# A graph network on one core: edge ranking in PSUM, counting shared with ScalarE, empty slots spread over many rows

## The chip, the cores and the metric

The kernel runs on one core of a Trainium2 chip. The metric is the device time of one execution in microseconds. Engines are named as in the profile: PE is TensorE, DVE is VectorE, ACT is ScalarE, POOL is GpSimd, SP is SyncE, which issues most transfers. An indirect DMA (a gather or a scatter with one row index per partition) is issued by POOL.

## What is computed

A graph of 6250 nodes with 64 features and 200000 edges, sorted by their target `dst`, goes through four blocks, each on a normalised copy of the node rows and added to them. Cut to what matters:

```python
h = relu(layernorm(x)); x = x + L0(h, W, b, edge_weight, src, dst)   # 3 hyperbolic GCN layers
h = relu(layernorm(x)); x = x + L1(h, edge_attr_16, ...)             # attention over edges
h = relu(layernorm(x)); x = x + L2(h, edge_attr_8, ...)              # edge MLP
h = relu(layernorm(x)); x = x + L3(h, ...)                           # attention over edges
# every block gathers node rows by src and sums over dst, for instance
msgs = edge_weight[:, None] * ht[src]
agg = segment_sum(msgs, dst, num_segments=6250)
```

So there are six passes over the edges: three GCN layers, attention, MLP, attention.

## The kernel before

**Buckets and groups.** The nodes are cut into T = 49 tiles of 128. An edge belongs to the bucket `dst >> 7`; bucket 49 takes the 704 entries that fill 200000 edges up to 128 x KC = 128 x 1568. Inside the chip the edges are sorted again by bucket (the kernel doesn't rely on their order), and each bucket is rounded up to groups of GE = 256 slots. NG = 832 groups are worked on. A slot that holds no edge has target NO_DST, which matches no node, and weight 0; its source is a node that doesn't exist, NO_SRC = 52 x 128 - 1, one row of the table for all empty slots.

**The sort**, in order. DVE fills a tile `fill` with empty slots, and SP writes it 42 times over the DRAM array `packed` (L283). The bucket of each edge is in `bucket`, 128 x 1568, in SBUF. *Counting* (L440 to L445): 50 times, once for each bin, DVE compares `bucket` with the bin and adds up along the row, into `cnt`. PE turns the counts into prefixes, and DVE into `base`, the next free position of each bin on each partition. *Ranking* (L474 to L497): the 1568 columns are done in portions of PLACED = 7, 14, 14, 14 units of 32 columns. For each portion 50 bins are gone through, five operations each: compare (a mask), running sum that starts at `base` (tensor_tensor_scan), its last column back to `base`, compare and multiply with the running sum, add to `rank`. Four closing operations turn the ranks into row numbers `pos`, and `pos_made` goes up.

**The scatter.** SP waits for `pos_made` of a portion and loads slabs of 16 columns of the payload and of `pos` (L292 to L301), two slabs in turn, each again when its 16 scatters have landed. POOL waits for all 42 fills and then scatters column by column into `packed`, 1568 indirect DMAs of 128 rows (L343). Meanwhile DVE does what comes before the first pass: the marks of the groups' first elements in RES (49 scalar_tensor_tensor of 832 columns), the layer input, the rows of layer 0. When all scatters have landed, SP loads `packed` in 42 pieces and DVE unpacks them. Then the first pass can begin.

**A pass.** POOL gathers the table rows of 256 slots by two indirect DMAs a group (L362), into a ring of 16 groups; SP loads the indices for 8 groups at a time, when the gathers of the turn before have landed. DVE makes one-hot matrices, PE multiplies them with the rows, and DVE adds the product to the node tile's sums ACC (L734 in GCN and MLP passes, L737 in attention passes). The loop has 16 groups a turn. Positions ascend with the bucket, so the groups that are left over at the end of the 832 hold empty slots alone.

## Time and profile before

| | us |
|---|---|
| median of 3 runs | 19662.9 |
| the runs | 19653.38 to 19730.66 |
| the profiled execution, its span | 16151.0 |
| POOL busy in it | 11150.9 (69%) |
| PE busy | 8811.1 (55%) |
| DVE busy | 8667.7 (54%) |
| ACT busy | 3544.5 (22%) |

The span reaches from the first to the last instruction of the profiled execution; the device times of the runs lie 3512 us above it, and the profile doesn't show what that is. The sort and the unpacking take the first 2569 us of the span, the six passes with the node work between them the rest. Busy shares are means over stages with different limits, so each stage has to be read by itself. POOL's time is almost all indirect DMAs, 1568 scatters and 9984 gathers.

### The profile page before, as it was taken

Reading aid. Unit: us, or ns where it says so; the run is one execution under the profiler, and the core shown is the slowest. Engines: PE = TensorE matmul, PEld = TensorE weight load, DVE = VectorE, ACT = ScalarE, POOL = GpSimd, SP = SyncE. Lnnn points to the kernel's source line nnn. Section 1 sums busy time; section 2 is a strip of 40 time slices with the busy share of each in tenths; the row PEclk is TensorE's granted clock in tenths of the full one; section 3 lists DMA queues with packets and bytes.
Section 4 is the critical chain, followed back from the end, with each engine's and each line's share of the span. In section 5 each row is a group of like instructions: output and inputs, shape, how many; then the busy total and the mean of one; then the engine's idle time right before and its main releaser. Section 6 shows DMA issues by size and latency. Waiting matters only on the chain.

```text
span 16151.0 us, 291712 instructions
## 1 busy us (share of the span) xinstructions
PE 8811.1 (55%) x60538; PEld 7573.0 (47%) x60539; DVE 8667.7 (54%) x38886; ACT 3544.5 (22%) x11877; POOL 11150.9 (69%) x11556
## 2 busy tenths in 40 slices
PE   0000002444434444434444488888699999788887
PEld 0000002333333333333333377777577777677777
DVE  8820004333343333343333488888766666688887
ACT  0000000000000000000000166666422222466665
POOL 3877774777747777747777477777477777477776
PEclk9965555555555555555555555555555555555555
DMA  2001113111121111221111211111211112211113
GB/s 86 20 24 26 26 31 83 27 27 27 27 21 27 27 27 27 26 23 27 27 27 27 22 27 26 26 26 26 21 27 27 26 26 26 20 28 27 27 27 27
DMA packets 509319, 465.87 MB, mean 29 GB/s; under 512 B 299149, under 2 KB 324301, under 8 KB 507854
## 3 DMA queue, kind: packets, MB, share of 16 engines
q0 software_dynamic: 369664, 358.70, 17.2%
q1 hardware_dynamic: 139086, 102.30, 2.2%
q14 instruction: 543, 4.45, 0.1%
q8 instruction: 26, 0.43, 0.0%
HBM read 389.08 MB, written 65.20 MB: 28 GB/s over the span
## 4 chain that ended last, share of the span: by engine, by line
PE 36%; DVE 23%; issue 21%; POOL 12%; DVEq 5%; DMA 3%; ACT 0%; POOLq 0%; ACTq 0%; SPq 0%
PE bank L1170 18%; POOL packed L343 10%; DVE OH L613 7%; PE bank L1269 6%; PE bank L1271 3%; DMA G<-table,idx 3%; DVE r_gm L646 2%; PE bank L1209 2%; PE bank L1282 2%; POOL G L362 2%; DVE ACC L734 1%; PE bank L1220 1%; PE bank L1232 1%; DVE ACC L737 1%; DVEq L596 1%
## 5 line engine op out<-in xcount | busy, mean ns | idle before, releaser
L362 POOL DMA_INDIRECT G<-table,idx x9984 | 9480.9, 950 | 4211.3 <-issue 2234.3
L1170 PE MATMUL bank<-G,OH 128*128 128x64 f32 x9984 | 2715.8, 428 | 5397.7 <-DVE OH L613 2605.1
L1170 PEld LDWEIGHTS bank<-G,OH 128*128 128x128 f32 x9984 | 2314.8, 322 | 5798.6 <-DVE OH L613 2897.2
L734 DVE TENSOR_TENSOR ACC<-ACC,bank 128x64 f32 (+1 forms) x3328 | 734.8, 221 | 3703.4 <-PE bank L1170 3701.6
L343 POOL DMA_INDIRECT packed<-Y,slab_pos x1568 | 1669.8, 1065 | 736.4 <-issue 494.7
L613 DVE TENSOR_SCALAR OH<-const,DL,W 128x128 f32<-128x128 f32 x4992 | 1740.1, 398 | 421.9 <-PE bank L1170 353.0
L1017 ACT ACTIVATE n_res<-n_arg 128x52 f32<-128x52 f32 x25 | 6.2, 246 | 8303.3 <-DVE n_arg L538 8179.8
L1170 PE MATMUL bank<-ZR,OH 128*128 128x65 f32 x6656 | 1765.4, 419 | 0.0
L1170 PEld LDWEIGHTS bank<-ZR,OH 128*128 128x128 f32 x6656 | 1623.9, 334 | 0.2
L1232 PE MATMUL bank<-ER,OHT 128*128 x9984 | 994.7, 174 | 751.1 <-DVE negm_lo L675 563.4
L1232 PEld LDWEIGHTS bank<-ER,OHT 128*128 128x128 bf16 x9984 | 781.8, 104 | 1048.5 <-issue 920.1
L1269 PE MATMUL bank<-WE,E8T 16*128 16x64 f32 x3328 | 1140.3, 443 | 41.6 <-ACT E8T L1092 41.4
L1220 PE MATMUL bank<-const,V 128*128 128x128 f32 x3328 | 1115.2, 439 | 21.9 <-ACT V L1072 21.8
L1209 PE MATMUL bank<-ident_b,OHB 128*128 128x128 bf16 x4992 | 1033.9, 311 | 39.1 <-DVE OHB L624 39.1
L624 DVE TENSOR_TENSOR OHB<-iota_b,DLw 128x256 bf16<-128x256 bf16 x2496 | 1051.4, 421 | 6.4 <-issue 6.4
L1269 PEld LDWEIGHTS bank<-WE,E8T 16*128 16x128 f32 x3328 | 828.1, 308 | 194.8 <-issue 50.4
L1047 ACT ACTIVATE OHT<-bank,const 128x256 bf16<-128x256 f32 x1664 | 785.2, 472 | 528.9 <-PE bank L1209 494.2
L1065 ACT ACTIVATE OH<-OHB,const 128x256 f32<-128x256 bf16 x1664 | 825.6, 496 | 41.1 <-DVE OHB L624 22.7
L417 DVE TENSOR_SCALAR W<-Z 128x40 f32 x42 | 8.1, 194 | 1494.7 <-DMA Z<-packed 1493.9
L1209 PEld LDWEIGHTS bank<-ident_b,OHB 128*128 128x128 bf16 x4992 | 656.2, 145 | 143.6 <-DVE OHB L624 39.9
L646 DVE TENSOR_REDUCE r_gm<-bank 128x1 f32<-128x256 f32 x1664 | 696.0, 418 | 9.1 <-PE bank L1220 8.8
L1047 ACT ACTIVATE OHT<-bank 128x256 bf16<-128x256 f32 x832 | 318.6, 383 | 1726.0 <-PE bank L1262 1722.0
(220 smaller groups left out, 14865.0 us busy)
## 6 DMA issues: line engine op xcount, KB each, us to landing
G<-table,idx POOLq DMA_INDIRECT x9984
packed<-Y SPq DMA_DIRECT2D x42, 640.0 KB, 17.5
Z<-packed SPq DMA_DIRECT2D x42, 640.0 KB, 3.7
Y<-in_payload SPq DMA_DIRECT2D x98, 256.0 KB
packed<-Y,slab_pos POOLq DMA_INDIRECT x1568
table<-Y SPq DMA_DIRECT2D x6, 1690.0 KB, 5.4
idx<-SRC SPq DMA_DIRECT2D x624, 8.0 KB
X<-in_x SPq DMA_DIRECT2D x1, 1568.0 KB, 8.7
```

The costliest lines, as they stand in the source:

```text
L343: pool.indirect_dma_start(out=packed_rows, out_offset=bass.IndirectOffsetOnAxis(ap=slab_pos[:, h, c:c + 1], axis=0), in_=slab[:, h, c, :], ...
L362: pool.indirect_dma_start(out=G[:, 2 * q + c, :], out_offset=None, in_=table, in_offset=bass.IndirectOffsetOnAxis(ap=idx[:, h, j:j + 1], a ...
L613: o = v.tensor_scalar(OH[:, q, c, :], iota, DL[:, at], W[:, at], ALU.is_equal, ALU.mult)
L624: v.tensor_tensor(OHB[:, q, :, :], iota_b[:, :].unsqueeze(1).to_broadcast([P, 2, P]), DLw[:, 2 * u:2 * u + 2].unsqueeze(2).to_broadcast([P ...
L646: v.tensor_reduce(sr["gm"][:, r:r + 1], ps_x[r % 2][:, 0:GE], AX.X, ALU.max).then_inc(a_done, 1)
L734: v.tensor_tensor(acc[:, 0:w], acc[:, 0:w], ps_a[r % 2][:, 0:w], ALU.add).then_inc(acc_done, 1)
L1047: return a.activation(OHT[:, r, :], ps_m[r % 2][:, 0:GE], ACT.Identity, scale=scale, bias=bias)
L1170: o = pe.matmul(ps_a[r % 2][:, 0:w], OH[:, q, c, :], parts[c], start=c == 0, stop=c == 1)
L1209: o = pe.matmul(ps_m[r % 2][:, c * P:(c + 1) * P], OHB[:, q, c, :], ident_b[:, :], start=True, stop=True)
L1220: o = pe.transpose(ps_x[r % 2][:, c * P:(c + 1) * P], V[:, r % 4, c, :], ident)
L1232: pe.matmul(e[:, c:c + 1], one, ER3[:, bass.ds(t, 1), k], start=k == 0, stop=k == 2)
L1269: pe.matmul(ps_e[r % 2][:, c * D:(c + 1) * D], E8T[:, r % 4, :], WE[:, c, :], start=True, stop=False)
```

## The change

Three things, in one edit. *Counting*: DVE counts the first 22 bins as before. ACT takes the other ACT_BINS = 28: it sums, in 29 passes over `bucket`, the sign of (middle of a bin - bucket), and half the difference of two such sums is the count of the bin between. *Ranking*: the mask and the running sum now lie in two PSUM banks instead of SBUF; `bucket` and `rank` stay in SBUF. A bank has 512 columns, so the portions are at most 480, and the first ones are small: PLACED = 2, 3, 5, 9, 15, 15. *Empty slots*: their source is one of the 384 nodes of the three tiles beyond the last, by partition and column, in `fill` and in the payload's last entries. Since these numbers come with the constants, the fill waits for them, and some clearing moves behind it.

```diff
-PLACED = [7, 14, 14, 14]
+PLACED = [2, 3, 5, 9, 15, 15]
+ACT_BINS = 28
...
-NO_SRC = TP * P - 1
+PAD_TILES = TP - T
...
-            sp.wait_ge(fill_made, 2)
+            sp.wait_ge(fill_made, 1)
...
-            sp.wait_ge(fill_made, 1)
+            sp.wait_ge(fill_made, 2)
...
             own.count(v.memset(y_flat[:, 0:PACK * PAY], 0.0))
-            own.wait()
-            own.count(v.memset(fill[:, :, SRC_AT:SRC_AT + 1].bitcast(I32), NO_SRC))
+            v.memset(WE[:, :, :], 0.0).then_inc(fill_made, 1)
+            own.wait()
+            v.wait_ge(s_const, 16)
+            for k in range(PAD_TILES):
+                to = fill[:, k:PACK:PAD_TILES, SRC_AT].bitcast(I32)
+                own.count(v.tensor_copy(to, pad_nodes[:, k:k + 1].to_broadcast([P, len(range(k, PACK, PAD_TILES))])))
+            own.wait()
             v.memset(fill[:, :, DST_AT:DST_AT + 1].bitcast(I32), NO_DST).then_inc(fill_made, 1)
-            v.memset(WE[:, :, :], 0.0).then_inc(fill_made, 1)
             own.count(v.memset(X[:, T:TP, :], 0.0))
             own.count(v.memset(sched[:, :], 0))
             own.count(v.memset(rank, 0.0))
-            v.wait_ge(s_const, 16)
...
-            with v.Fori(0, NB) as b:
+            with v.Fori(0, low) as b:
...
+            v.wait_ge(signs_summed, ACT_BINS + 1)
+            tt(cnt[:, low:NB], sums[:, low:NB], sums[:, low - 1:NB - 1], ALU.subtract)
+            ts(cnt[:, low:NB], cnt[:, low:NB], 0.5, None, ALU.mult)
...
+                ps_mask, ps_scan = bank[3][:, 0:c1 - c0], bank[4][:, 0:c1 - c0]
...
-                    ts(mask[:, here], bucket[:, here], one, None, ALU.is_equal)
+                    ts(ps_mask, bucket[:, here], one, None, ALU.is_equal)
                     own.wait()
-                    own.count(v.tensor_tensor_scan(scan[:, here], ones[:, 0:1].to_broadcast([P, c1 - c0]), mask[:, here],
+                    own.count(v.tensor_tensor_scan(ps_scan, ones[:, 0:1].to_broadcast([P, c1 - c0]), ps_mask,
                                                    carry, ALU.mult, ALU.add))
                     own.wait()
-                    own.count(move(carry, scan[:, c1 - 1:c1]))
-                    stt(mask[:, here], bucket[:, here], one, scan[:, here], ALU.is_equal, ALU.mult)
-                    tt(rank[:, here], rank[:, here], mask[:, here], ALU.add)
+                    own.count(move(carry, ps_scan[:, c1 - c0 - 1:c1 - c0]))
+                    stt(ps_mask, bucket[:, here], one, ps_scan, ALU.is_equal, ALU.mult)
+                    tt(rank[:, here], rank[:, here], ps_mask, ALU.add)
...
+            a.wait_ge(s_const, 16)
+            a.wait_ge(bucket_made, 1)
+            for j in range(ACT_BINS + 1):
+                b = NB - ACT_BINS - 1 + j
+                need(a, signs_summed, j - 1)
+                a.activation(signs[:, j % 2, :], bucket, ACT.Sign, scale=-1.0, bias=mids[:, b:b + 1],
+                             accum_out=sums[:, b:b + 1]).then_inc(signs_summed, 1)
...
+    c[:, C_PAD:C_PAD + PAD_TILES] = np.arange(T * P, TP * P).reshape(PAD_TILES, P).T
+    c[:, C_MID:C_MID + NB] = np.arange(NB) + 0.5
...
-    payload[N_EDGES:, SRC_AT] = NO_SRC
+    payload[N_EDGES:, SRC_AT] = T * P + np.arange(P * KC - N_EDGES) % (PAD_TILES * P)
```

On DVE, one turn of the loop over the bins in the first portion, before (EA8 is the memory in which `bucket`, the mask, the running sum and `rank` lie; a scan is listed as a SCALAR_TENSOR_TENSOR):

```order
L405 TENSOR_SCALAR EA8<-EA8,const 128x224
L74 REGISTER_ALU
L482 ISA [waits dve_done]
L482 SCALAR_TENSOR_TENSOR EA8<-const,base,EA8 128x224
L74 REGISTER_ALU
L417 TENSOR_SCALAR base<-EA8 128x1 [waits dve_done]
L74 REGISTER_ALU
L409 SCALAR_TENSOR_TENSOR EA8<-EA8,const 128x224 [waits dve_done]
L74 REGISTER_ALU
L401 TENSOR_TENSOR EA8<-EA8 128x224 [waits dve_done]
```

The same turn in the changed kernel:

```order
L413 TENSOR_SCALAR bank3<-EA8,const 128x64
L77 REGISTER_ALU
L498 ISA [waits dve_done]
L498 SCALAR_TENSOR_TENSOR bank4<-const,base,bank3 128x64
L77 REGISTER_ALU
L425 TENSOR_SCALAR base<-bank4 128x1 [waits dve_done]
L77 REGISTER_ALU
L417 SCALAR_TENSOR_TENSOR bank3<-EA8,const,bank4 128x64 [waits dve_done]
L77 REGISTER_ALU
L409 TENSOR_TENSOR EA8<-EA8,bank3 128x64 [waits dve_done]
```

The order is the same; the mask moved to bank 3 and the running sum to bank 4, and the portion shrank from 224 to 64 columns.

On ACT, the start of its stream, before (fn_arg is DVE's request for a function on node values):

```order
L1017 ACT_TABLE_LOAD
L1017 ACTIVATE hb_r<-hb_arg 128x3 [waits fn_arg]
L1017 ACT_TABLE_LOAD
L1017 ACTIVATE hb_t<-hb_norm 128x3 [waits fn_arg]
L1017 ACT_TABLE_LOAD
```

And in the changed kernel:

```order
L1122 ACT_TABLE_LOAD [waits bucket_made]
L1122 ACTIVATE EA8,sums<-EA8,const 128x1568 [waits s_const]
L1122 ACTIVATE EA8,sums<-EA8,const 128x1568
L1122 ACTIVATE EA8,sums<-EA8,const 128x1568 [waits signs_summed] x27
L1033 ACT_TABLE_LOAD
L1033 ACTIVATE hb_r<-hb_arg 128x3 [waits fn_arg]
```

The 29 sums stand ahead of all that ACT did, and start when DVE has made the buckets; DVE waits for them ahead of the prefixes.

## Rows read from the trace of the kernel before

**Rows 1.** The page's head and its chain that ended last, by engine.

```profile
span 16151.0 us, 291712 instructions
PE 36%; DVE 23%; issue 21%; POOL 12%; DVEq 5%; DMA 3%; ACT 0%; POOLq 0%; ACTq 0%; SPq 0%
```

**Rows 2.** Windows: stretch, length, busy of PE, PEld, DVE, ACT, POOL; clock, DMA, GB/s.

```profile
110.00:237.00 127.00, 2.20 (x10) 2.00 (x10) 105.42 (x270) 0.00 (x0) 0.00 (x0) 1.00 0.00 0
...
570.00:740.00 170.00, 0.00 (x0) 0.00 (x0) 150.74 (x247) 0.00 (x0) 138.99 (x100) 1.00 0.08 20
...
1100.00:2400.00 1300.00, 0.00 (x0) 0.00 (x0) 0.00 (x0) 0.00 (x0) 976.49 (x1021) 0.50 0.11 26
```

**Rows 3.** First count in time; by form: compares of two widths, one from PSUM.

```profile
8.08 1.84 DVE L443 TENSOR_SCALAR_CACHE_REDUCE EA<-EA,const 128x1568 f32<-128x1568 f32 x1 [0.20 <-DVE EA L436]
...
L405 DVE TENSOR_SCALAR EA<-EA,const 128x224 f32<-128x224 f32 x50 | 16.8, 336 | 7.6 <-DVE EA L401 7.5
...
L405 DVE TENSOR_SCALAR EA<-EA,const 128x448 f32<-128x448 f32 x98 | 44.5, 454 | 14.8 <-DVE EA L401 14.8
...
L417 DVE TENSOR_SCALAR ACC<-bank 128x256 f32 x12 | 5.1, 425 | 18.5 <-PE bank L1152 18.5
```

**Rows 4.** Timeline (start, duration, what): count done, ranking, second portion, scatters.

```profile
110.17 0.19 DVE L447 COPY base<-cnt 128x50 f32<-128x50 f32 x1
...
114.98 0.34 DVE L405 TENSOR_SCALAR EA<-EA,const 128x224 f32<-128x224 f32 x1
...
236.84 0.45 DVE L405 TENSOR_SCALAR EA<-EA,const 128x448 f32<-128x448 f32 x1
...
242.19 1.12 POOL L343 DMA_INDIRECT packed<-Y,slab_pos  x1 [241.72 <-DMA slab_pos<-EA]
...
2405.76 0.96 POOL L343 DMA_INDIRECT packed<-Y,slab_pos  x1 [0.30 <-issue]
```

**Rows 5.** Timeline and groups: indirect DMAs beside DVE work with different operands.

```profile
833.69 3.63 DVE L401 TENSOR_TENSOR U<-X,n_a 128x3328 f32<-128x3328 f32 x1
833.97 4.17 POOL L343 DMA_INDIRECT packed<-Y,slab_pos  x1 [0.31 <-issue]
...
L409 DVE SCALAR_TENSOR_TENSOR RES<-V,cum,RES 128x832 f32<-128x832 f32 x49 | 54.5, 1113 | 6.5
...
L343 POOL DMA_INDIRECT packed<-Y,slab_pos x45 | 43.8, 974 | 15.1 <-issue 15.1
...
4520.55 0.94 POOL L362 DMA_INDIRECT G<-table,idx  x1 [0.30 <-PE bank L1170]
4520.62 0.22 DVE L734 TENSOR_TENSOR ACC<-ACC,bank 128x64 f32 x1 [1.58 <-PE bank L1170]
```

**Rows 6.** ACT groups by form, whole span: count, busy and mean ns, idle before.

```profile
L1065 ACT ACTIVATE OH<-OHB,const 128x256 f32<-128x256 bf16 x1664 | 825.6, 496 | 41.1 <-DVE OHB L624 22.7 <-PE bank L1170 18.4
...
L1072 ACT ACTIVATE V<-OHB,G 128x128 f32<-128x128 bf16 x1664 | 564.6, 386 | 29.9 <-DMA G<-table,idx 28.3 <-PE bank L1220 1.6
```

**Rows 7.** ACC on DVE: windows (busy, clock, DMA, GB/s), then its attention timeline.

```profile
4590.00:4673.00 83.00, 5.32 (x24) 0.50 0.89 19
4300.00:4383.00 83.00, 7.32 (x33) 0.50 0.19 27
...
11640.00:13690.00 2050.00, 174.39 (x790) 0.50 0.18 27
13715.00:13790.00 75.00, 6.59 (x30) 0.50 0.76 16
...
11417.12 0.28 DVE L737 SCALAR_TENSOR_TENSOR ACC<-ACC,r_corr,bank 128x65 f32 x1
11425.73 0.28 DVE L737 SCALAR_TENSOR_TENSOR ACC<-ACC,r_corr,bank 128x65 f32 x1
...
11460.88 0.28 DVE L737 SCALAR_TENSOR_TENSOR ACC<-ACC,r_corr,bank 128x65 f32 x1
...
11484.35 0.28 DVE L737 SCALAR_TENSOR_TENSOR ACC<-ACC,r_corr,bank 128x65 f32 x1
```

More of the change, by code:

```diff
@@ L58 @@
 assert STEPS_N % 2 == 1
-assert sum(PLACED) * 2 * SLAB == KC and NS % PACK == 0 and (NS // PACK) % 2 == 0 and KC % (2 * SLAB) == 0
+assert max(PLACED) * 2 * SLAB <= 512 and sum(PLACED) * 2 * SLAB == KC and NS % PACK == 0 and (NS // PACK) % 2 == 0 and KC % (2 * SLAB) == 0
 assert NS * P >= NG * GE + P * KC - N_EDGES + GE and P * SCHED >= NG + BODY
 C_ID, C_TRI, C_IOTA, C_ONE, C_BIN, C_GRP = 0, P, 2 * P, 3 * P, 4 * P, 4 * P + NB
-C_ALL = C_GRP + SCHED
+C_PAD = C_GRP + SCHED
+C_MID = C_PAD + PAD_TILES
+C_ALL = C_MID + NB
 B_GCN, B_BIAS, B_GAMMA, B_BETA, B_B1, B_B2, B_BIAS3 = 0, 3, 4, 5, 6, 7, 8
@@ L114, in build @@
         ea8_flat = EA8[:, :, :].rearrange("p s c -> p (s c)")
-        bucket, mask, scan, rank, posf = (ea8_flat[:, i * KC:(i + 1) * KC] for i in range(5))
+        bucket, mask, signs, rank = (ea8_flat[:, i * KC:(i + 1) * KC] for i in range(4))
+        signs = signs.bitcast(BF16).rearrange("p (h c) -> p h c", h=2)
         dst_raw = ea8_flat[:, 5 * KC:6 * KC].bitcast(I32)
@@ L130, in build @@
         grp_i = sb("grp_i", [P, NB], I32)
+        sums = sb("sums", [P, NB])
         before = sb("before", [P, SCHED, T])
@@ L139, in build @@
         bins, groups = const[:, C_BIN:C_BIN + NB], const[:, C_GRP:C_GRP + SCHED]
+        pad_nodes = const[:, C_PAD:C_PAD + PAD_TILES]
+        mids = const[:, C_MID:C_MID + NB]
         ident_b = sb("ident_b", [P, P], BF16)
@@ L209, in build @@
         counted, prefixes = sem("counted"), sem("prefixes")
+        bucket_made, signs_summed = sem("bucket_made"), sem("signs_summed")
         sched_made, sched_stored, sched_loaded = sem("sched_made"), sem("sched_stored"), sem("sched_loaded")
@@ L435, in _ @@
             own.wait()
-            own.count(v.tensor_scalar(bucket, pos_hi, float(T), None, ALU.min))
+            v.tensor_scalar(bucket, pos_hi, float(T), None, ALU.min).then_inc(bucket_made, 1)
+            v.wait_ge(bucket_made, 1)
+            low = NB - ACT_BINS
             at0 = own.n
-            with v.Fori(0, NB) as b:
+            with v.Fori(0, low) as b:
                 own.n = b + at0
@@ L444, in _ @@
                                           accum_out=cnt[:, bass.ds(b, 1)]))
-            own.n = at0 + NB
+            own.n = at0 + low
+            v.wait_ge(signs_summed, ACT_BINS + 1)
+            tt(cnt[:, low:NB], sums[:, low:NB], sums[:, low - 1:NB - 1], ALU.subtract)
+            ts(cnt[:, low:NB], cnt[:, low:NB], 0.5, None, ALU.mult)
             own.wait()
```

## Prediction

> **What bounds the kernel now.** I read the page's head and its chain first. The profiled span is 16151.0 us and no engine owns the chain: PE, DVE, POOL and plain issue share it [rows 1]. The change touches two stretches only, so the question is what ends last in each, and the busy shares say nothing on that. The median of the runs is 19662.9 us, 3512 us above the span; nothing in the trace lies in those 3512 us. I make the sum on the span and take the rest as it is, with one rival for the case that it isn't.
>
> The first stretch is the sort. Read the windows in order. GpSimd's scatter of the payload starts at 242.19 and its last one at 2405.76; only then does SyncE load the packed edges, and the passes come after that [rows 4]. From 1100 on VectorE does nothing [rows 2]. So the stretch is: when the first scatter starts, plus 1568 scatters at their pace. The pace has two values: 1021 scatters in 1300 us where VectorE is idle, 1.273 us each, and 100 in 170 us while VectorE ranks, 1.70 us each [rows 2]. At 1.273 us throughout, 1567 steps would take 1995 us; they took 2163.6, so 168 us are lost to VectorE's work. The 519 us of ranking after 242 hold 305 scatters at 1.70, 0.427 us too many each: 130 us. The other 38 us belong to work after the ranking, which stays.
>
> The second stretch is the end of each of the six passes. Each pass takes 832 groups of 256 slots. 200000 edges fill 782 groups, and each of 49 buckets rounds up by half a group on average, so some 25 groups at the end hold empty slots alone, all pointing at one row of the table. There the sums on ACC come 24 times in 83 us against 33 times before, and the DMA share is 0.89 against 0.19 [rows 7].
>
> **The change, part by part.** *Counting.* It begins at 8.08 and its result is copied at 110.17: 50 bins at 2.04 us, of which 1.84 is the operation [rows 3, 4]. VectorE keeps 22, 45 us. It starts later, since the clearing of rank and two smaller ones now stand behind the wait for the constants: I allow 3 us for them, so 11 to 56. ScalarE does 29 passes over 1568 columns, a form that isn't in the trace. Its forms with a pointer bias take 386 ns for 128 columns and 496 ns for 256 [rows 6]: 0.86 ns a column, so 496 + 1312 x 0.86 = 1.62 us, plus a gap and a read of the accumulator of 0.1 to 0.3 us as VectorE shows (2.04 against 1.84). I take 1.8: 29 are 52 us, with a table load the count ends near 65, and ScalarE is the later of the two. The bounds are 56 (ScalarE hidden behind VectorE) and 80 (2.3 us each). Two small operations more, then as before 4.81 us to the ranking [rows 4]: it starts at 70.3, not at 114.98, 44.7 us earlier.
>
> The Trainium skill, ScalarE: Activation LUTs, section What ACT_TABLE_LOAD costs, gives an activation with pointer bias about 280 ns + 0.833 ns a column: an estimate of 1.59 us, by which the count would end some 6 us sooner. No row here shows it at this width.
>
> *Ranking.* Before, a bin over 224 columns takes (236.84 - 114.98 - 1.3)/50 = 2.41 us (1.3 for the four closing operations) and over 448 columns 3.44, 247 instructions at five a bin in 170 us [rows 2, 4]: 1.37 us + 4.62 ns a column. With PSUM the compare loses its speed: it takes 336 ns and 454 ns in SBUF, 0.53 ns a column; the nearest tensor_scalar with a PSUM operand takes 425 ns for 256 columns, at best 1.06 ns a column [rows 3]. Slope 5.15 ns. For the fixed part that row shows nothing extra; I take 1.42 us, bounds 1.37 and 1.70. Portions of 64, 96, 160, 288, 480, 480 columns give 1.75, 1.91, 2.24, 2.90, 3.89, 3.89 us a bin, thus 87, 96, 112, 145, 195, 195 us, 830 in all with 6 us of closing work, against some 647 before. Those 190 us more of VectorE lie beside the scatters: ranking ends near 906 and what follows is done well before the scatters are. The cover is over 1000 us.
>
> That the compare slows is what the rows show; VectorE: DVE Perf Modes of the Trainium skill, section Why PSUM operands drop a tier, states it as a rule, and it speaks against the change. By it and by the row the first portion is 64 x 0.53 x 50 = 1.7 us longer than in SBUF; only the sum over all columns, 42 us, would hurt, and that is covered.
>
> *First scatter.* The first positions come at 70.3 + 87 + 1 = 158.8, and the scatter starts 5.35 us behind them as before (236.84 to 242.19 [rows 4]): 164.2, a gain of 78 us.
>
> *Starving.* 64 columns keep GpSimd busy for 81.5 us, to 245.7. The next positions come at 158.8 + 97 = 255.8, and with 5.35 us for the loads GpSimd waits 15.4 us. The 96 columns then last until 383; the third positions come at 369, so nothing is waited for, with 9 us to spare; later portions have more. Cost 15 us, bounds 0 and 45 (fixed part at 1.70 us a bin: both gaps open).
>
> *The pace beside the ranking.* A tensor_tensor of 3.63 us with both inputs in SBUF holds a scatter that began behind it for 4.17 us, to 0.82 us after its end. But 49 scalar_tensor_tensor with both inputs in SBUF leave 45 scatters at 974 ns. An ACC sum with one input in PSUM runs inside a gather of 0.94 us and adds nothing [rows 5]. In the new ranking no operation has two tensor inputs in SBUF and the compare doesn't write SBUF. So I take 1.273: the 130 us go. The bounds are 0 and 130; I am near the upper one since the PSUM row is the same kind of operation.
>
> SBUF — State Buffer in the Trainium skill, section Who interferes with whom, says that an operation with at most one SBUF input outside the two-port modes doesn't contend with GpSimd. By that rule the 130 us go too. It also counts any operation with two SBUF inputs as contending; the 974 ns row doesn't bear that out.
>
> *Empty slots.* In a GCN pass 3.46 us a group against 2.52 over some 26 groups: 25 us, three times 75 [rows 7]. In an attention pass the last but one turn of the loop has a gap of 23.5 us between ACC sums where others have 8.6 (11417.12 to 11425.73): 15 us [rows 7]; the other such pass has the same shape, I take 13. In the MLP pass 30 sums in 75 us against 790 in 2050 [rows 7]: nothing to win. Together 103 us. The fill gets three small operations more, hidden: GpSimd waits for its transfers too, but from 110 us on the DMAs carry nothing [rows 2], and the first scatter comes 54 us later still.
>
> **Sum.** 78 + 130 - 15 = 193 for the sort and 103 for the slots: 296 us. Span 15855, time 19367.
>
> **Rivals.** *The contention stays* (PSUM doesn't keep VectorE out of GpSimd's way, or it is the compare or the scan that blocks in any place). Then scatters run at 1.70 for 906 - 164 = 742 us: 436 of them, 186 us lost, no starving. The sort gains 78 + 130 - 186 = 22, with the slots 125: 19538. Against it stand the ACC rows, for it that these are short, 0.22 us.
>
> *Scatters fall in step with the bins, and the kernel is slower.* Before, two scatters fit each bin of 3.44 us. If only one went through per bin, wherever its gap is, 742 us of ranking would hold 250 scatters: 742 - 250 x 1.273 = 424 us lost, the sort 216 us later, the whole 113 us slower after the slots: 19776. It decides from a mean pace of 2.2 us on. The widest bins, 3.9 us, are where it would show. Against it: even a fully blocked scatter ends 0.82 us after the blocker [rows 5], and no blocker of that length is left.
>
> *The slots win nothing*, since the slow pace at the end has another cause: 193 us, 19470. The DMA share of 0.89 at 19 GB/s against 27 [rows 7] speaks against it: slower descriptors, not more bytes.
>
> *The 3512 us lie in the indirect DMAs*: over 11552 of them, 0.30 us each. Then gathers set 3.1 us a group everywhere, the slots win about 10 us a pass, and the blocking may be partly hidden: 105 to 240 us, say 19490.
>
> **Chances.** Forecast 0.68; contention stays 0.10; slots nothing 0.07; time in the DMAs 0.11; slower 0.04. For the range: at the top 19540, which takes in the first, third and fourth rival; at the bottom, if the gain grows with 19663/16151, 360 us: 19300. Faster or slower counts from 0.5%, 98 us, about what a measurement of this kernel can tell from no change. Below 19565 lie the forecast, two rivals whole and most of the others: 0.92; within 0.05; slower 0.03.
>
> **What would show it.** First scatter near 164, one gap of about 15 us some 80 us later, then about 0.96 us a scatter all through the ranking, last scatter near 2213. ScalarE's passes near 1.6 to 1.8 us. No rise of the DMA share at the ends of the passes, ACC sums at 2.5 us there. Wrong if scatters still take 1.3 to 1.5 us beside the ranking, if GpSimd waits at the third portion too, or if span and time don't shrink alike.

## The result, and the profile after

| | us |
|---|---|
| before, median of 4 runs beside the changed kernel | 19659.8 |
| changed kernel, median of 4 runs | 19877.2 (19836.6 to 19897.2) |
| ratio, 95% interval | 1.0088 (1.0061 to 1.0115) |
| profiled execution of the changed kernel | 19862.0, span 19860.2 |

Predicted were 19367 us and a range of 19300 to 19540: 296 us less. It is 217 us more.

One thing has to be said first, since no number can be read without it: chips differ. On some, the kernel before takes 16.1 ms, on others 19.7 to 19.9 ms, and its span is then as long as its time. I call them **A chips** and **B chips**. The trace of before [rows 1 to 7] is from an A chip, the times under it from B chips, and so is the result. What the prediction called "3512 us above the span" lies inside the span of a B chip. Only kernels on chips of one kind are compared below.

Head and chain of the page after (against [rows 1]), two of its groups, and what GpSimd's scatters waited for from 100 to 2650 us (waited for, sum, times, longest):

```profile
span 19860.2 us, 293015 instructions
...
PE 19%; another core or an unknown queue 17%; issue 11%; DVE 11%; DVEq 4%; ACT 2%; ACTq 0%; DMA 0%; POOL 0%; SPq 0%; POOLq 0%
...
L370 POOL DMA_INDIRECT G<-table,idx x9984 | 9619.5, 963 | 7595.1 <-issue 2888.1
L750 DVE TENSOR_TENSOR ACC<-ACC,bank 128x64 f32 (+1 forms) x3328 | 732.2, 220 | 5514.6 <-remote 3968.0
...
POOL packed L351 <- DMA slab_pos<-EA: 491.4, 5, 158.8
```

Five waits for positions where I forecast two. The first, 158.8 us, is the time to the first scatter; the other four are 333 us, and I had allowed 15.

The timeline of VectorE and ScalarE after, where the count ends and ranking starts (start, duration, engine, what, idle before):

```profile
52.13 0.08 DVE L455 DVE_READ_ACCUMULATOR EA<-EA,const  x1
53.26 1.59 ACT L1122 ACTIVATE EA<-EA,const 128x1568 bf16<-128x1568 f32 x1
54.75 0.19 ACT L1122 ACTIVATION_READ_ACCUMULATOR EA<-EA,const 128x1 f32 x1
54.84 1.59 ACT L1122 ACTIVATE EA<-EA,const 128x1568 bf16<-128x1568 f32 x1
...
56.55 0.19 DVE L409 TENSOR_TENSOR cnt<-sums 128x28 f32<-128x28 f32 x1 [2.30 <-ACT EA L1122]
...
61.79 0.29 DVE L413 TENSOR_SCALAR bank<-EA,const 128x64 f32<-128x64 f32 x1
...
159.25 1.12 POOL L351 DMA_INDIRECT packed<-Y,slab_pos  x1 [158.78 <-DMA slab_pos<-EA]
```

Up to here all is as forecast, 5 us early. Now the second portion (96 columns), first while the scatters have just begun, then 40 us later:

```profile
172.32 0.32 DVE L413 TENSOR_SCALAR bank<-EA,const 128x96 f32<-128x96 f32 x1 [0.46 <-issue]
174.50 0.32 DVE L413 TENSOR_SCALAR bank<-EA,const 128x96 f32<-128x96 f32 x1 [0.46 <-DVE EA L409]
178.45 0.32 DVE L413 TENSOR_SCALAR bank<-EA,const 128x96 f32<-128x96 f32 x1 [2.23 <-issue]
...
211.38 0.32 DVE L413 TENSOR_SCALAR bank<-EA,const 128x96 f32<-128x96 f32 x1 [4.08 <-issue]
214.74 0.42 DVE L498 TENSOR_TENSOR_SCAN bank<-const,base,bank 128x96 f32<-128x96 f32 x1 [3.04 <-issue]
216.14 0.16 DVE L425 TENSOR_SCALAR base<-bank 128x1 f32 x1 [0.98 <-DVE bank L498]
217.54 0.32 DVE L417 SCALAR_TENSOR_TENSOR bank<-EA,const,bank 128x96 f32<-128x96 f32 x1 [1.24 <-issue]
218.95 0.25 DVE L409 TENSOR_TENSOR EA<-EA,bank 128x96 f32<-128x96 f32 x1 [1.08 <-issue]
223.98 0.32 DVE L413 TENSOR_SCALAR bank<-EA,const 128x96 f32<-128x96 f32 x1 [4.77 <-issue]
```

The compare comes again after 2.18 us at 174.50 and after 12.60 us at 223.98. The operations are as long as before (0.32, 0.42, 0.16); what grew is the idle time ahead of them, put down to "issue": nothing that the profile shows was waited for. (This trace holds 98480 records of semaphore updates where that of [rows 1] has 255417, and so it is with every trace of a B chip. So the names of what ended a wait are less sure here, and I go by the starts.) When GpSimd has run out of positions (from 239 to 326.8), VectorE is back at 2.2 us a bin. So the small portions make GpSimd wait, its waiting frees VectorE, and its next scatters hold VectorE again.

### The profile page after: what moved, and what is told of

It is laid out like the page before. It is cut to its first block, busy times and chain, and to the rows that moved or that the text cites. A ratio compares the mean times of both kernels' runs of the same rounds, so it can differ in the third digit from the quotient of the medians.

```text
span 19860.2 us, 293015 instructions
## 1 busy us (share of the span) xinstructions
PE 9006.6 (45%) x60538; PEld 7528.7 (38%) x60539; DVE 8505.1 (43%) x39342; ACT 3392.3 (17%) x11936; POOL 11213.2 (56%) x11556
## 4 chain that ended last, share of the span: by engine, by line
PE 19%; another core or an unknown queue 17%; issue 11%; DVE 11%; DVEq 4%; ACT 2%; ACTq 0%; DMA 0%; POOL 0%; SPq 0%; POOLq 0%
PE bank L1193 6%; PE bank L1243 4%; PE bank L1255 3%; PE bank L1232 2%; PE bank L1292 2%; DVE OH L629 2%; DVEq L612 2%; PE bank L1259 1%; DVE OHB L640 1%; DVE r_gm L662 1%; PE bank L1294 1%; DVE ACC L753 1%; ACT V L1088 1%; DVE ACC L750 1%
## 5 line engine op out<-in xcount | busy, mean ns | idle before, releaser
L370 POOL DMA_INDIRECT G<-table,idx x9984 | 9619.5, 963 | 7595.1 <-issue 2888.1
L1193 PE MATMUL bank<-G,OH 128*128 128x64 f32 x9984 | 2599.3, 431 | 5022.8 <-DVE OH L629 2471.4
L1193 PEld LDWEIGHTS bank<-G,OH 128*128 128x128 f32 x9984 | 2265.0, 324 | 5357.1 <-DVE OH L629 2472.9
L351 POOL DMA_INDIRECT packed<-Y,slab_pos x1568 | 1593.5, 1016 | 998.4 <-issue 507.0
L629 DVE TENSOR_SCALAR OH<-const,DL,W 128x128 f32<-128x128 f32 x4992 | 1551.5, 359 | 516.5 <-issue 468.9
L1168 PE MATMUL bank<-const,st 128*64 128x128 f32 x728 | 146.3, 370 | 2277.7 <-ACT st L1042 2277.7
L1168 PEld LDWEIGHTS bank<-const,st 128*64 128x64 f32 x728 | 118.5, 191 | 2286.8 <-issue 2068.4
```

Source lines behind the costliest of these rows:

```text
L351: pool.indirect_dma_start(out=packed_rows, out_offset=bass.IndirectOffsetOnAxis(ap=slab_pos[:, h, c:c + 1], axis=0), in_=slab[:, h, c, :], ...
L370: pool.indirect_dma_start(out=G[:, 2 * q + c, :], out_offset=None, in_=table, in_offset=bass.IndirectOffsetOnAxis(ap=idx[:, h, j:j + 1], a ...
L629: o = v.tensor_scalar(OH[:, q, c, :], iota, DL[:, at], W[:, at], ALU.is_equal, ALU.mult)
L1193: o = pe.matmul(ps_a[r % 2][:, 0:w], OH[:, q, c, :], parts[c], start=c == 0, stop=c == 1)
```

## The experiments

All durations of a bin below are from start to start of its running sum. Each run's comparison is with the kernel before on the same chip.

**Each part alone, on an A chip** (before: 16135 us).

> The kernel before, unchanged, looked at once more. The trace that the prediction was made on has a span of 16151 us, while the runs took 19660; the changed kernel's span (19860) is its whole time. Theory A (engines are held at issue while GpSimd issues indirect DMAs, before the change too): the span is near 19650, the passes take 2400 us and more as in the changed kernel, and VectorE's ranking beside the scatters shows idle time put down to issue. Theory B (only the changed kernel has these idle times): the span is near 16150 again and the 3500 us lie outside it.

Measured: time 16099.4, span 16097.6 us, scatters from 241.5 to 2405.7. The trace of [rows 4] again, and no 3512 us beside the span.

> The kernel before with only the empty slots spread over 384 rows. Theory A (the end of each pass is held by one row): 103 us faster as predicted, 0.5%; less if all passes are slower than the trace of before showed, since then the tail is no slower than the rest: 0 to 60 us faster. Theory B (the slots are what slows the changed kernel): slower by some 200 us.

```diff
-    payload[N_EDGES:, SRC_AT] = NO_SRC
+    payload[N_EDGES:, SRC_AT] = T * P + np.arange(P * KC - N_EDGES) % (PAD_TILES * P)
```

Measured: ratio 0.9937 (0.9916 to 0.9957), 129 us by the medians, 90 between the two traces. Windows at the end of the first GCN pass, before and with the slots spread (columns as in [rows 2]):

```profile
4600.00:4660.00 60.00, 19.48 (x72) 16.68 (x72) 14.66 (x54) 0.00 (x0) 38.79 (x42) 0.50 0.87 20
```

```profile
4600.00:4660.00 60.00, 26.15 (x98) 22.32 (x98) 20.53 (x70) 0.00 (x0) 43.64 (x47) 0.50 0.17 26
```

The DMA share of 0.87 is gone and 47 gathers fit in 60 us where 42 did; in both windows the last 3 us hold no gather, as the pass has none left. More is won behind the last gather. Its issue and the last sum on ACC of this pass, before and with the slots spread:

```profile
4657.25 0.96 POOL L362 DMA_INDIRECT G<-table,idx  x1 [0.30 <-issue]
4676.50 0.22 DVE L734 TENSOR_TENSOR ACC<-ACC,bank 128x64 f32 x1 [2.65 <-PE bank L1170]
```

```profile
4656.71 0.94 POOL L364 DMA_INDIRECT G<-table,idx  x1 [0.30 <-issue]
4660.52 0.22 DVE L739 TENSOR_TENSOR ACC<-ACC,bank 128x64 f32 x1 [2.34 <-PE bank L1175]
```

The sum comes 19 us behind the gather in the first and 4 us in the second. From first gather to last sum the GCN passes take 22.7, 22.4 and 21.8 us less, 67 in all (forecast 75), the attention passes 27 and 24 (forecast 15 and 13), the MLP pass the same. The attention figures move by 15 us and more between kernels with the same slots. The forecast of 103 us lies between 129 and 90. What lies between the passes moves in steps of some 21 us from trace to trace and adds up to 560 to 624 us whatever the kernel, so two single spans can differ by some 60 us for that alone.

> The kernel before with only the mask and the running sum of the ranking in PSUM, portions of 224 and 448 columns kept. Theory A (port contention is what PSUM takes away): scatters beside the ranking take 0.96 us instead of 1.3 to 1.5, up to 130 us faster. Theory B (VectorE is held at issue beside the scatters, so GpSimd's pace no longer hangs on it): within 60 us of before.

```diff
-                    ts(mask[:, here], bucket[:, here], one, None, ALU.is_equal)
+                    ts(ps_mask, bucket[:, here], one, None, ALU.is_equal)
...
-                    tt(rank[:, here], rank[:, here], mask[:, here], ALU.add)
+                    tt(rank[:, here], rank[:, here], ps_mask, ALU.add)
```

Measured: 0.9929 (0.9906 to 0.9952), 130 us, last scatter at 2282.3. The timeline while scatters run:

```profile
699.47 0.69 DVE L405 TENSOR_SCALAR bank<-EA,const 128x448 f32<-128x448 f32 x1 [0.15 <-DVE EA L401]
700.29 1.15 DVE L483 TENSOR_TENSOR_SCAN bank<-const,base,bank 128x448 f32<-128x448 f32 x1
701.48 0.16 DVE L417 TENSOR_SCALAR base<-bank 128x1 f32 x1
701.67 0.69 DVE L409 SCALAR_TENSOR_TENSOR bank<-EA,const,bank 128x448 f32<-128x448 f32 x1
702.39 0.62 DVE L401 TENSOR_TENSOR EA<-EA,bank 128x448 f32<-128x448 f32 x1
703.17 0.69 DVE L405 TENSOR_SCALAR bank<-EA,const 128x448 f32<-128x448 f32 x1 [0.15 <-DVE EA L401]
```

A bin is 3.71 us and scatters pass at 1.27 each. From the first scatter to the last it is 2033.5 us, 2164.3 in e0: the 130 us of blocking are gone, and the rival "contention stays" is out. The first scatter comes 7 us later (248.8), which leaves 124 us at the first gather; the medians differ by 130, the two spans by 91.

> The kernel before with only the counting shared with ScalarE. The first scatter comes some 50 us earlier. Theory A: that goes through to the end, 50 us faster (0.25%). Theory B (what follows eats it): no difference, or slower.

```diff
-            with v.Fori(0, NB) as b:
+            with v.Fori(0, low) as b:
...
+            v.wait_ge(signs_summed, ACT_BINS + 1)
```

Measured: 0.9954 (0.9932 to 0.9975), 80 us; first scatter 187.0 in place of 241.5. The first gather comes 46 us earlier and the span is 57 us shorter, near the 44.7 us forecast; the 80 us of the medians are more than the trace accounts for, and the eight times spread over 125 us. So on an A chip each part wins about what its term said.

**The same chip, a B chip, for before, after and between** (before: 19938 us).

> The kernel before once more, for a trace from the same chip as the next three. Two conditions are known so far. In the one (16.1 ms for this kernel) the scatters run from 241.5 to 2359 or 2406 and VectorE's ranking bins over 448 columns take 3.44 us. In the other (19.66 ms) there is no trace of this kernel yet. My theory of it: while GpSimd issues indirect DMAs, the instructions of the other engines are held before they start. It expects ranking bins of 9 us or more once the scatters have begun, most of it as idle time put down to issue, and gather passes of 2.6 to 3.1 ms in place of 2.08. The rival, that each indirect DMA is simply 0.3 us longer on that chip, expects bins of 3.4 us and a uniformly slower scatter.

Measured: 19952.5, span 19950.7 us. Its groups beside the scatters, 240 to 2520 us, and the gathers:

```profile
L482 DVE TENSOR_TENSOR_SCAN EA<-const,base,EA 128x448 f32<-128x448 f32 x150 | 172.6, 1151 | 20.8
L409 DVE SCALAR_TENSOR_TENSOR RES<-V,cum,RES 128x832 f32<-128x832 f32 x49 | 53.7, 1096 | 131.8 <-issue 129.2
...
L362 POOL DMA_INDIRECT G<-table,idx x9984 | 9605.2, 962 | 7776.9 <-issue 2805.0
```

My theory of it failed in half. The passes are held: 2432 to 3193 us each where the A chip takes 2081 to 2254, in sum 16472 against 12780; that is nearly all of the 3853 us between the two spans. The 49 marks in RES are held too, 131.8 us of idle where the A chip shows 6.5 [rows 5]. But the ranking of the kernel before is not: bins of 3.47 us, on both kinds of chip alike. There the scatters, at 1.73 us, are the ones that are blocked.

> The changed kernel as it is. If this chip is one on which the kernel before takes 16.1 ms: the three parts alone gave 129, 130 and 80 us, so the whole should give about 300 us, 15830 us, ratio 0.981, with the last scatter near 2210 and at most 15 us of waiting GpSimd after the first portion. If it is one of 19.66 ms: ratio 1.009 again, because VectorE is held between its instructions while scatters are issued, and the small portions leave GpSimd without positions for some 330 us. The rival (the gather passes are what got slower, by the slots' table rows) expects the loss in the passes and not before 2600 us.

Measured: 1.0047 (1.0032 to 1.0062). Scatters from 159.2 to 2606.6, GpSimd waits 344 us after the first; ranking bins at 12.6 us beside the scatters, whatever their width.

> The changed kernel with the old portions of 224 and 448 columns; slots, PSUM and the shared count stay. Where before takes 16.1 ms: first scatter near 187, the sort some 20 us later than with small portions, 15850 us, ratio 0.982. Where it takes 19.66 ms: if the starved GpSimd is the cause of the loss, most of the 330 us come back, 19500 to 19600 us, ratio 0.992 to 0.997, and GpSimd waits for positions less than 100 us; if the loss lies elsewhere (the PSUM operands, the passes) the ratio stays at 1.009.

```diff
-PLACED = [2, 3, 5, 9, 15, 15]
+PLACED = [7, 14, 14, 14]
```

Measured: 0.9974 (0.9962 to 0.9986), 164 us better than the change. GpSimd still waits once after the first scatter, 101.6 us (295.7 less the 194.1 before any scatter), as the bins are held here too. Groups over 60 to 1250 us, and the waits:

```profile
L498 DVE TENSOR_TENSOR_SCAN bank<-const,base,bank 128x448 f32<-128x448 f32 x109 | 125.8, 1154 | 173.5 <-issue 167.9 <-DVE bank L413 0.6
L413 DVE TENSOR_SCALAR bank<-EA,const 128x448 f32<-128x448 f32 x109 | 74.9, 687 | 336.8 <-issue 330.7 <-DVE EA L409 6.1
...
POOL packed L351 <- DMA slab_pos<-EA: 295.7, 2, 194.1
```

Bins of 448 columns take 12.6 us, as those of 96 do. The width doesn't matter; so a portion costs 630 us beside scatters, and fewer portions mean less waiting.

> The kernel before with the small portions alone; rank through SBUF, VectorE counts all, the slots point at one row. Where before takes 16.1 ms: the first scatter comes at about 170 in place of 241.5 (-71), GpSimd waits once or twice for some 10 us, contention stays at 1.7 us a scatter over 250 us more of ranking: 50 to 70 us faster or nothing, ratio 0.995 to 1.000. Where it takes 19.66 ms: 300 to 400 us slower, ratio 1.015 to 1.02, if starving is the cause, since nothing else of the change is in it; 1.000 or below if the small portions are innocent.

The edit is the one line of e6, the other way round, on the kernel before. Measured: 1.0066 (1.0044 to 1.0087). So narrow bins are held without PSUM too: with everything in SBUF, bins of 96, 160 and 288 columns take about 12.6 us as well, and only those of 480 run at 3.61 with scatters at 1.8. Wide bins are another matter: over 448 columns they run at 3.47 us through SBUF (e4) and at 12.6 through PSUM (e6). Smaller portions alone make the kernel slower on a B chip.

**What in a bin is held.** The next four went first to an A chip (before: 16123 us), and show there what each is worth when nothing is held.

> The kernel before with the spread slots and the shared count, ranking as before (SBUF, portions of 224 and 448 columns). The theory is that only the ranking of the changed kernel loses where the kernel before takes 19.7 to 19.9 ms: there the first scatter comes 55 us earlier, ranking bins keep their 3.47 us and nothing is held, so 55 us from the count and some 20 to 30 from the slots: ratio 0.9960 (0.9945 to 0.9975). Where before takes 16.1 ms: 80 + 129 us less whatever the two share, ratio 0.987 to 0.990. The rival, that a held VectorE can come with any earlier start, expects bins of 12.6 us here as well and a ratio of 1.00.

Its edits are those of e1 and e3 together. Measured: 0.9875 (0.9849 to 0.9900).

> All three parts with portions of 224 and 448 columns, as in e6, but the 50 bins of a portion are written out one after the other, so that VectorE waits on constants and has no loop counter, no register and no branch there. In e6 on the chip of 19.9 ms each bin over 448 columns took 12.6 us in place of 3.8. If registers and branches are what is held: bins of 3.9 us, no waiting GpSimd, last scatter near 2180, ratio 0.984 to 0.987 against 0.9974. If every instruction that waits on and raises a semaphore is held, whatever it waits for: bins stay at 12.6 us, ratio 0.997. In between (the branch alone): the largest gap, before the compare, goes and bins take 8 to 9 us. Where before takes 16.1 ms nothing of this shows: bins 3.7 us, ratio 0.981 to 0.983 either way.

```diff
-                with v.Fori(0, NB) as b:
-                    own.n = b * 5 + at0
-                    one, carry = bins[:, bass.ds(b, 1)], base[:, bass.ds(b, 1)]
+                for b in range(NB):
+                    one, carry = bins[:, b:b + 1], base[:, b:b + 1]
```

Measured: 0.9826 (0.9803 to 0.9849); bins 3.48 us.

> The changed kernel with its small portions, bins written out as in e9. If registers and branches are held: bins of 1.8 to 4 us beside the scatters, GpSimd waits 15 us at the second portion as I had forecast, last scatter near 2160 and ratio 0.983 on the slower chip (the changed kernel had 1.0047 there). If every instruction is held: 1.005 again. Where before takes 16.1 ms: as the changed kernel, 0.981.

Measured: 0.9797 (0.9772 to 0.9822), 336 us, the best on an A chip. First scatter 140.5, one wait of 3.5 us after it, last scatter 2173.0.

> The kernel of e6 with a sixth instruction in each bin, a tensor_scalar over 128x1 that takes 0.16 us (it multiplies a used number by one into a tile that is no longer read). On the slower chip a bin of five took 12.6 us beside ten scatters. If each of VectorE's instructions costs two scatters or 2.5 us, a bin takes 15.1 us; if a bin is held as a whole, or by the branch alone, it stays at 12.6 to 12.8. Where before takes 16.1 ms the bin goes from 3.71 to 3.90 us.

```diff
+                    ts(grp[:, 0:1], cum[:, 0:1], 1.0, None, ALU.mult)
```

Measured: 15904 us, bins 4.09 us. Then a B chip (before: 19687 us).

> The changed kernel, which has been timed only where the kernel before takes 19.7 to 19.9 ms (1.0088 and 1.0047). Where before takes 16.1 ms nothing holds VectorE in the runs so far, and my sum for the span should stand there: 296 us less, 15.82 ms, ratio 0.9815 (0.978 to 0.985), first scatter at 159, GpSimd waits once for 5 to 20 us after it, last scatter near 2210. If this is a chip of 19.7 to 19.9 ms: ratio 1.003 to 1.010 for the third time.

Measured: 1.0092 (1.0075 to 1.0109), 194 us.

> The changed kernel with its ranking bins written out (e10 again; there 0.9797 where before takes 16.1 ms). On a chip of 19.9 ms: if registers and branches are what is held, bins of 1.6 to 3.6 us beside the scatters, GpSimd waits under 20 us, last scatter near 2170 to 2280, ratio 0.981 to 0.985. If every instruction that waits on and raises a semaphore is held, as long as in a loop: bins of 12.6 us, the starving stays and the ratio is 1.003 to 1.010.

Measured: 0.9950 (0.9927 to 0.9974), 83 us. Bins beside scatters 7.0 us; GpSimd waits 140 us in three waits after the first scatter, and the last scatter is at 2406.0.

> The same with portions of 224 and 448 columns (e9 again; 0.9826 where before takes 16.1 ms). On a chip of 19.9 ms: registers and branches held: bins of 3.5 us, no starving, ratio 0.984 to 0.987; every instruction held: bins of 12.6 us, 296 us of starving as in e6, ratio 0.997.

Measured: 0.9912 (0.9895 to 0.9930), 172 us, with bins of 7.0 us, no waiting after the first scatter and the last one at 2349.1. (The 296 us of e6 in this text count the wait for the first scatter too; 102 was meant.)

> e6 with a sixth instruction of 0.16 us in each bin (e11 again; there the bin went from 3.71 to 4.09 us, 0.38 for it with its wait). On a chip of 19.9 ms: 15.1 us a bin if each instruction costs about two scatters, 12.6 to 12.8 if the bin is held as a whole or by its branch.

Measured: 19757.9 us, bins of 14.0. The timelines of f3, then f4:

```profile
702.09 1.16 DVE L497 TENSOR_TENSOR_SCAN bank<-const,base,bank 128x448 f32<-128x448 f32 x1 [0.72 <-DVE bank L413]
703.48 0.16 DVE L425 TENSOR_SCALAR base<-bank 128x1 f32<-128x1 f32 x1 [0.23 <-DVE bank L497]
704.88 0.69 DVE L417 SCALAR_TENSOR_TENSOR bank<-EA,const,bank 128x448 f32<-128x448 f32 x1 [1.24 <-DVE base L425]
706.27 0.62 DVE L409 TENSOR_TENSOR EA<-EA,bank 128x448 f32<-128x448 f32 x1 [0.71 <-DVE bank L417]
707.69 0.69 DVE L413 TENSOR_SCALAR bank<-EA,const 128x448 f32<-128x448 f32 x1 [0.79 <-DVE EA L409]
```

```profile
702.77 1.16 DVE L498 TENSOR_TENSOR_SCAN bank<-const,base,bank 128x448 f32<-128x448 f32 x1 [2.74 <-issue]
704.17 0.16 DVE L425 TENSOR_SCALAR base<-bank 128x1 f32 x1 [0.24 <-issue]
705.58 0.69 DVE L417 SCALAR_TENSOR_TENSOR bank<-EA,const,bank 128x448 f32<-128x448 f32 x1 [1.25 <-issue]
706.98 0.62 DVE L409 TENSOR_TENSOR EA<-EA,bank 128x448 f32<-128x448 f32 x1 [0.71 <-issue]
709.08 0.15 DVE L413 TENSOR_SCALAR grp<-cum 128x1 f32<-128x1 f32 x1 [1.48 <-issue]
714.04 0.69 DVE L413 TENSOR_SCALAR bank<-EA,const 128x448 f32<-128x448 f32 x1 [4.81 <-issue]
```

Read the starts. In f3 they are 1.39, 1.40, 1.39, 1.42 us apart, though the operations last 1.16, 0.16, 0.69 and 0.62: nearly each of VectorE's instructions takes 1.40 us beside the scatters, and five of them 7.0. In f4's loop the distances are 1.40, 1.41, 1.40 and 2.10, and from the last operation over the branch to the next compare 4.96. In a turn of the loop with five operations nine further instructions stand (registers, the parts of the scan and compare that are issued apart, the branch); they make the bin 12.6 instead of 7.0, 5.6 us. The sixth operation, with one register instruction more, adds 1.40, not the 2.5 that I had put on it. So both of my readings were half right: every instruction is held, and those of the loop on top.

**The last two,** on another B chip (before: 19680 us).

> The changed kernel once more, for the case that the kernel before takes 16.1 ms on this chip: then my sum for the span is tested with nothing held. It gave 296 us less; e10, which differs in the written out bins alone, gave 336. Expected 290 to 310 us less, ratio 0.981 to 0.982, first scatter at 159, GpSimd waits 5 to 20 us after the first portion, last scatter near 2200. If before takes 19.7 to 19.9 ms: 1.005 to 1.009 again.

Measured: 1.0078 (1.0062 to 1.0095).

> Spread slots and shared count with the ranking of before (e8 again, 0.9875 where before takes 16.1 ms). If before takes 19.7 to 19.9 ms here: bins of 3.47 us, not held, and no starving; 55 us from the count and 20 to 40 from the slots, ratio 0.9950 to 0.9965, against 0.9974 for the three parts with large portions and 1.005 to 1.009 for the change as it is. If an earlier start alone brings the holding: bins of 12.6 us and 0.998 to 1.005. If before takes 16.1 ms: 0.9875 again.

Measured: 0.9966 (0.9944 to 0.9989), bins 3.47 to 3.59 us. The two parts that leave the ranking alone win 74 us where the whole change loses 155. The three parts with large portions (e6, 0.9974, on another B chip) won no more: the PSUM ranking in a loop frees the scatters there but gets VectorE held. The last scatter comes at 2445 in e6 and at 2465 in g2, the first gather at 2695 and at 2644.

## Why the prediction was wrong

**The step that failed** is the one on the first lines: "nothing in the trace lies in those 3512 us", and then "I make the sum on the span and take the rest as it is". The 3512 us are not beside the span. On a B chip the span is 19950.7 us (e4), and the difference lies between the instructions of VectorE, TensorE, ScalarE and GpSimd while indirect DMAs are issued. The rival that put them in the indirect DMAs, 0.30 us each, had the place right and the effect mostly wrong: most of it is the other engines being stretched. In numbers, the six passes take 3692 us more (16472 against 12780) and the stretch ahead of them 121 (first gather at 2693.8 against 2572.4). A part of those 121 us is the scatters' own. Windows of e4 and e0 in which VectorE does nothing:

```profile
1800.00:2400.00 600.00, 0.00 (x0) 0.00 (x0) 0.00 (x0) 0.00 (x0) 447.14 (x428) 1.00 0.10 23
1800.00:2400.00 600.00, 0.00 (x0) 0.00 (x0) 0.00 (x0) 0.00 (x0) 450.83 (x472) 0.50 0.10 26
```

That is 1.40 us a scatter on the B chip and 1.27 on the A chip, though the middle one is 0.96 us long on both. So the span of an A chip gives the cost of VectorE beside scatters for A chips alone; of the bins here only the wide ones in SBUF cost the same on both. In the sum, the terms that this broke are the starving and the cover.

**Point by point,** with the ledger of one B chip (e4 against e5, both traced):

| | forecast | measured |
|---|---|---|
| first scatter | -78 | -83.6 (242.8 to 159.2) |
| GpSimd starved | +15 | +344 |
| scatters no longer blocked | -130 | -168 |
| work that was to be covered | 0 | +64 |
| six passes and what lies between | -103 | -62 |
| sum | -296 | +95 (spans 19950.7 and 20045.6) |

*First scatter: right, 5 us early, by two errors that partly cancel.* Ranking starts at 61.79 instead of 70.3, and its first portion takes 4.5 us more than I said. ScalarE's pass was forecast at 1.62 us and, with its gap, 1.8; it is 1.59, and the next starts 1.58 us behind it, since the read of the accumulator overlaps it. The estimate of 1.59 us for that width, worked out from the formula in ScalarE: Activation LUTs of the Trainium skill, section What ACT_TABLE_LOAD costs, is what the trace shows.

*The narrow bins: somewhat too low even where nothing is held.* 64 columns took 1.84 us after (forecast 1.75), 96 took 2.18 until 175 us (forecast 1.91); 160, 288 and 480 took 2.24, 2.88 and 3.87 (forecast 2.24, 2.90, 3.89). With 50 bins of 2.18 us GpSimd would have waited some 29 us instead of 15 (an estimate: they start at 154.8, from the end of the first portion's bins to its first scatter it is 5.9 us, and GpSimd runs dry at 240.4). The 1.06 ns a column for the compare is right (0.32 us at 96 columns and 0.69 at 448 give 1.05), but the row of 425 ns doesn't give it: less the 218 ns that the two rows in SBUF leave at no columns, it gives 0.81.

*Starving: the term that broke the sum.* Its upper bound of 45 us came from a dearer fixed part. The real bin was 12.6 us once held, so 50 such bins last 630 us, while the portions of 64 to 288 columns keep GpSimd busy for 81 to 366; after each of these four it ran dry.

*The blocked scatters: right.* 130 forecast, 131 timed in e2. Of the 168 on the B chip 134 lie in the ranking of the kernel before (302 scatters up to 761.9 us, against 1.2735 us each). Against the same pace the rest of e4's scatters lose 142 us and all of e5's 108 beside the waits, where an A chip loses 38; the other 34 are the difference, and much of both is the 1.40 us pace shown above. The rule that I weighed, in SBUF — State Buffer of the Trainium skill, section Who interferes with whom, is that an operation with at most one SBUF input, outside the two-port modes, doesn't contend. It held in e2 with scatters at 1.27 us beside 448 columns. Its other half, on two SBUF inputs, the page limits to GpSimd instructions that read SBUF, which my text left out; the scatters of the 974 ns row take `slab_pos` from there.

*The cover: wrong.* "The cover is over 1000 us" counted on a ranking that ends near 906. Its last running sum starts at 1807, and then come the 49 marks in RES. The group over 1800 to 2850 us, the end of the preparation in the timeline, and what SyncE waited for meanwhile:

```profile
L417 DVE SCALAR_TENSOR_TENSOR RES<-V,cum,RES 128x832 f32<-128x832 f32 x49 | 53.2, 1085 | 217.3 <-issue 217.3
...
2671.17 0.19 DVE L906 COPY n_e<-n_r 128x52 f32<-128x52 f32 x1
2675.69 0.19 DVE L425 TENSOR_SCALAR W<-Z 128x40 f32 x1 [4.33 <-DMA Z<-packed]
...
SPq L313 <- DVE n_e L906: 115.0, 1, 115.0
```

The preparation ends at 2671, 80 us behind the last scatter at 2591.4; SyncE loads the packed edges only then, and VectorE unpacks behind it. From the last scatter to the first gather the kernel before takes 179.3 us (e4); after, it takes 245.4, and 243.7 in e5. In f3, where the last running sum starts at 1170, it is 179.5 again.

*The slots: right on an A chip, smaller on a B chip.* Of the 62 us, 22 lie between the passes, where one step is 21; in the passes e5 is 40 us shorter than e4, next to nothing of it in the GCN passes. The one-row table is as slow there, but so is everything. Windows in the first pass of e4, its end and its middle:

```profile
5065.00:5125.00 60.00, 22.51 (x90) 19.89 (x90) 17.20 (x66) 0.00 (x0) 39.65 (x42) 1.00 0.86 20
4800.00:4860.00 60.00, 25.04 (x96) 21.84 (x96) 19.02 (x71) 0.00 (x0) 39.78 (x42) 1.00 0.15 23
```

The DMA share is 0.86 against 0.15, and 42 gathers are issued in 60 us either way: the slow rows hide behind GpSimd, which is itself held. The same rows have a granted clock of 1.00 where the A chip has 0.50 and is faster, so TensorE's clock is not what makes the B chip slow.

**What stays open.** Why chips differ, and which path the other engines share with GpSimd's indirect DMAs: the runs show that each instruction waits, in steps near 0.70 us, not on what. It isn't only those with a semaphore: in the loop of the changed kernel three register instructions that wait on nothing start at 219.59, 221.00 and 222.39 us (they are in the trace, though its views leave them out). Holding doesn't set in at once either: 14 to 48 us after the scatters start or resume in the loops, 24 to 77 where the bins are written out. By then VectorE has each time done what would take it 57 to 107 us more at the held pace (an estimate: the time until then, times held bin over free bin less one). That would fit something that fills up first; no run tests it. One rival stands untested: every time on record comes with a span and a granted clock from the profiler, and each trace of a B chip holds 95000 to 101000 records of semaphore updates where each of an A chip holds 255000 to 257000, so the recording itself may be what holds the engines. Also open is why wide bins in SBUF (448 and 480 columns) are never held, and narrow ones are. The changed kernel itself didn't meet an A chip. There e10, the same with the bins written out, won 336 us, and its first scatter came 18.7 us sooner than the change's; that the change would win some 300 there, as the sum said, is an estimate and wasn't measured.

**Better than both.** The three parts with portions of 224 and 448 columns and written out bins (e9, f3): 0.9826 on an A chip and 0.9912 on a B chip. With the small portions (e10, f2) it is 0.9797 and 0.9950, so the portions should be chosen for the chip on which the kernel will run. (On the A chip the two intervals overlap; the last scatter comes at 2211.6 with large portions and 2173.0 with small ones.)

## What to carry to other kernels

When the time of the runs and the span of the trace differ by a fifth, the trace may be from other conditions, as here: settle that before any sum, since a term that is hidden in the one may be bare in the other. Cutting work into small portions to start a consumer early pays only if the producer keeps its pace once the consumer runs; take its pace from beside the consumer, in the worst condition known, and multiply by the number of portions. Where VectorE works beside indirect DMAs on such a chip, count its instructions and not its columns, and write short loops out (e6 to f3: 0.9974 to 0.9912).

## What the runs showed of the hardware

- On B chips an instruction of VectorE beside back-to-back scatters takes 1.40 us from start to start, be it 0.16 or 1.16 us long. A loop turn of five tensor operations takes 12.6 us, of six 14.0; written out, five take 7.0. On A chips the same are 3.71, 4.09 and 3.48 us. In the changed kernel holding sets in 16 us after the first scatter (159.25 to 175) and ends when GpSimd runs dry.
- VectorE operations that block the scatters (SBUF, 448 columns) aren't held themselves: 3.47 us a bin on both kinds of chip. The same bin through PSUM is 3.71 on an A chip and 12.6 on a B chip.
- Scatters alone, with VectorE idle, come 1.27 us apart on an A chip (472 in 600 us) and 1.40 in the same stretch on a B chip (428).
- A loop costs 0.23 us a bin of 448 columns even where nothing is held (3.71 against 3.48) and 0.36 a bin of 64 (1.84 against 1.48), which is 18 of the 18.7 us by which e10's first scatter comes sooner.
- Gathers in which all 128 rows are one row of the table drive the DMA share to 0.87; at the end of a pass on an A chip 42 are issued in 60 us in place of 47, and the last sum comes 19 us behind the last gather in place of 4.
